# Attention scores made transposed in column halves on TensorE, turned by VectorE in 32x32 blocks, with the row statistics exchanged between partition quarters

## The reference, cut to what matters

```python
q = (query @ wq).reshape(bs, sq, 32, 128)     # query: x, normalised
k = (key @ wk) ...; v = (value @ wv) ...      # key, value: ctx; each kv head serves 4 query heads
q, k = rope(q), rope(k)
raw = einsum('bhqd,bhkd->bhqk', q, k) / sqrt(128) + mask
attn = softmax(raw, axis=-1)                  # over the 64 keys of the same sequence
x = x + tanh(g) * (attn @ v) @ wo
```

## Time and profile before

| | us |
|---|---|
| median of three runs | 782.57 |
| profiled execution, its own time | 782.34 |
| its span (first to last instruction) | 780.5 |
| PE busy | 770.2 |
| DVE busy | 561.7 |
| POOL busy | 498.7 |
| ACT busy | 421.6 |

### The profile page before, as it was taken

The page is one execution under the profiler, slowest core; times in us unless marked ns, Lnnn a source line. Parts: engine busy times, 40 slices in busy tenths (PEclk is TensorE's granted clock), DMA queues, the critical chain, the costliest instruction groups (busy, mean ns, idle before and its releaser), DMA issues.

```text
span 780.5 us, 13547 instructions
## 1 busy us (share of the span) xinstructions
PE 770.2 (99%) x4845; PEld 628.6 (81%) x4845; DVE 561.7 (72%) x1072; ACT 421.6 (54%) x796; POOL 498.7 (64%) x431
## 2 busy tenths in 40 slices
PE   8999999999999999999999999999999999999998
PEld 7888888888888888888888888888656777777776
DVE  6868876677777556677655656656999987998874
ACT  5754454433444433343444324332779898888773
POOL 2798477655567764556776545655377876887752
PEclk9999999999999999999999999999999999999999
DMA  9315645554633343352244311357163323113101
GB/s 338 111 41 136 182 109 133 159 119 120 171 105 105 107 129 103 92 162 86 88 105 133 105 38 55 67 164 280 44 173 96 96 61 93 53 49 82 47 16 41
DMA packets 94798, 85.70 MB, mean 110 GB/s; under 512 B 50652, under 2 KB 66236, under 8 KB 94348
## 3 DMA queue, kind: packets, MB, share of 16 engines
q1 hardware_dynamic: 94444, 84.51, 38.0%
q10 hardware_dynamic: 288, 0.33, 0.1%
HBM read 56.38 MB, written 13.68 MB: 90 GB/s over the span
## 4 chain that ended last, share of the span: by engine, by line
PE 91%; DVE 4%; ACT 1%; POOL 1%; SPq 1%; issue 1%; DMA 0%; DVEq 0%; POOLq 0%
PE bank L81 12%; PE bank L83 11%; PE bank L82 11%; PE bank L583 7%; PE bank L606 7%; PE bank L601 7%; PE bank L602 7%; PE bank L697 4%; PE bank L1699 4%; PE bank L1685 3%; PE bank L1651 2%; PE bank L1630 2%; PE bank L1622 2%; PE bank L1675 2%; PE bank L1676 2%; PE bank L1662 1%
## 5 line engine op out<-in xcount | busy, mean ns | idle before, releaser
L1007 DVE SCALAR_TENSOR_TENSOR x_res<-bank,gate,x_res 128x512 f32<-128x512 f32 x128 | 95.5, 747 | 71.4 <-PE bank L606 70.8
L1278 POOL TENSOR_TENSOR prob<-prob,row_inv 128x512 f32<-128x512 f32 x32 | 33.5, 1046 | 154.6 <-DVE row_inv L996 154.6
L1264 POOL TENSOR_TENSOR rope_swap<-rope_swap,trig 128x512 f32<-128x512 f32 x80 | 104.2, 1302 | 29.2 <-ACT rope_swap L767 28.8
L893 ACT CAST oT_hi<-bank 128x512 fp32r<-128x512 f32 x64 | 34.4, 590 | 162.4 <-PE bank L697 162.4
L766 ACT COPY rope_swap<-bank 64x512 f32<-64x512 f32 x80 | 46.8, 585 | 111.3 <-DVE rope_cos L971 111.3
L601 PE MATMUL bank<-wo_hi,oT_hi 128*128 128x512 f32 x256 | 101.5, 397 | 0.6 <-issue 0.5
L81 PE MATMUL bank<-xnT_hi,wq_hi 128*128 128x512 f32 x252 | 101.7, 404 | 0.0
L602 PE MATMUL bank<-wo_lo,oT_hi 128*128 128x512 f32 x256 | 100.9, 394 | 0.0
L83 PE MATMUL bank<-xnT_hi,wq_lo 128*128 128x512 f32 x252 | 99.7, 395 | 0.0
L82 PE MATMUL bank<-xnT_lo,wq_hi 128*128 128x512 f32 x252 | 99.5, 395 | 0.0
L971 DVE TENSOR_TENSOR rope_cos<-bank,trig 128x512 f32<-128x512 f32 x80 | 54.1, 677 | 56.3 <-PE bank L83 54.1
(11 more groups left out here) (276 smaller groups left out, 1887.7 us busy)
## 6 DMA issues: line engine op xcount, KB each, us to landing
wq_raw<-in_wq_tiles SPq DMA_DIRECT2D x16, 512.0 KB, 3.8
wo_raw<-in_L_xattn_wo SPq DMA_DIRECT2D x16, 512.0 KB, 3.9
blocks_dram<-blocks SPq DMA_DIRECT2D x28, 256.0 KB, 2.0
probT<-blocks_dram SPq DMA_DIRECT2D x112, 64.0 KB, 2.0
xn<-in_L_ffn_Wd SPq DMA_DIRECT2D x16, 256.0 KB, 2.9
b_ctx<-in_ctx SPq DMA_DIRECT2D x32, 128.0 KB, 2.7
b_k_twice<-b_qk_hi SPq DMA_DIRECT2D x32, 128.0 KB, 2.4
w_T_dram<-w_out SPq DMA_DIRECT2D x28, 128.0 KB, 3.1
```

Of the source, the lines that this page charges most:

```text
L1007: dve.scalar_tensor_tensor(out=K.x[:, t, :], in0=wo_ps[t % 2][:, :], scalar=K.gate[:, 0:1], in1=K.x[:, t, :], op0=ALU.mult, op1=ALU.add).t ...
L1264: pool.tensor_tensor(out=sw, in0=sw, in1=sin_b, op=ALU.mult).then_inc(s_rope, 1)
```

## The change

Scores are made the other way round: the keys are stationary (64 columns) and (head, query) moves (128 columns), and the two sequences of a tile go to the two halves of the output partitions. DVE turns the 32x32 blocks of the scores, so that queries (32 of them) lie on partitions and keys along the row, but a query's 64 keys are in two neighbouring partition quarters. Maximum and sum are therefore taken over 32 keys each, and exchanged between neighbouring quarters by four copies of 32 rows x 16 columns, each time followed by a joint maximum or sum. A second turn of the blocks gives the transposed weights directly in `probT`; the transposes on PE and the way through DRAM go. The conversion of weight pieces moves from DVE to ACT, and the order of DVE's and POOL's programs changes: `normalise` stands behind the first rotation, the turn back behind the first accumulation, the low parts of the heads are apart. In slots 0 and 1 PE does items earlier.

```diff
+NROW = HALF // QB
...
-        mask = sb("mask", [P, B, S])
+        mask = sb("mask", [P, UNITS, HALF])
...
-            def blocks_out(U):
...
-            def blocks_in(U):
...
@@ score_unit (PE) @@
-                    pe.wait_ge(s_soft, 5 * (U - 1) + 1)
-                for n in range(2 * UT):
-                    b = 2 * UT * u + n
-                    mm = pe.matmul(score[:, n * S:(n + 1) * S], q_rope[jp][:, b], k_rope[:, b * S:(b + 1) * S],
-                                   start=True, stop=True)
+                    pe.wait_ge(s_soft, soft(U - 1, TURNED))
+                for tl in range(UT):
+                    for par in range(2):
+                        b = 2 * (UT * u + tl) + par
+                        mm = pe.matmul(score[par * S:(par + 1) * S, tl * P:(tl + 1) * P], k_rope[:, b * S:(b + 1) * S],
+                                       q_rope[jp][:, b], start=True, stop=True)
@@ slot (PE) @@
+            def slot(g, last, jp, u, U, items):
+                lead = {0: len(items), 1: 1}.get(U, 0)
+                if U == 1:
+                    item(*items[0])
+                if U > 0:
+                    output(U - 1)
...
+                    score_unit(g if (jp, u) != (1, UNITS - 1) else g + 1, *next_unit(jp, u))
+                if U == 0:
+                    for G, pos in items:
+                        item(G, pos)
+                values(g, jp, u, U)
+                for G, pos in items[lead:]:
                     item(G, pos)
@@ body (ACT) @@
                     if (p := piece_at(2 * U - 1)) is not None:
                         shift(p)
+                        to_int(p)
...
+                    if U > 0:
+                        attended(U)
                     if U < 2 * NPAIR - 1:
                         exp_unit(U + 1)
+                    for G, pos in items[0:1]:
+                        evacuate(G, pos)
...
+                    if (p := piece_at(2 * U)) is not None:
+                        to_int(p)
@@ DVE @@
+            def swap_halves(U, step):
+                dve.wait_ge(s_soft, soft(U, step))
+                for q in range(NQ):
+                    mine, other = slice(q * QB, (q + 1) * QB), slice((q ^ 1) * QB, ((q ^ 1) + 1) * QB)
+                    dve.tensor_copy(row_other[other, U % 2, :], row_max[mine, U % 2, :]).then_inc(s_swap, 1)
             def soft_first(U):
...
+                dve.transpose(pr, score[:, :]).then_inc(s_soft, 1)
+                dve.wait_ge(s_soft, soft(U, TURNED))
+                dve.scalar_tensor_tensor(out=pr, in0=pr, scalar=float(1.0 / np.sqrt(np.float32(DH))), in1=mask[:, u, :],
+                                         op0=ALU.mult, op1=ALU.add).then_inc(s_soft, 1)
+                dve.wait_ge(s_soft, soft(U, MASKED))
+                dve.tensor_reduce(out=row_max[:, u, :], in_=prob[u][:, :, :], op=ALU.max, axis=AX_X).then_inc(s_soft, 1)
+            def soft_shift(U):
+                u = U % 2
+                swap_halves(U, MAX_OWN)
+                dve.wait_ge(s_swap, swapped(U, 1))
+                dve.tensor_tensor(out=row_max[:, u, :], in0=row_max[:, u, :], in1=row_other[:, u, :], op=ALU.max).then_inc(s_soft, 1)
+                dve.wait_ge(s_soft, soft(U, MAX_BOTH))
+                dve.tensor_tensor(out=prob[u][:, :, :], in0=prob[u][:, :, :],
+                                  in1=row_max[:, u, :].unsqueeze(2).to_broadcast([P, NROW, QB]), op=ALU.subtract).then_inc(s_soft, 1)
             def soft_sum(U):
...
+            def soft_inverse(U):
...
+                swap_halves(U, SUM_OWN)
...
+            def turn_back(U):
                 dve.wait_ge(s_prob, U + 1)
+                dve.transpose(probT[:, :, :].rearrange("p t n -> p (t n)"), prob[U % 2][:, :, :].rearrange("p r c -> p (r c)")
+                              ).then_inc(s_probT, 1)
@@ slot (DVE) @@
                 for k in range(UT):
+                    T = UT * (U - 1) + k
+                    accumulate(T, T % NT)
...
+                    if k == 0:
+                        turn_back(U)
+                    if k == 1 and (p := piece_at(2 * U)) is not None:
                         find_scale(p)
...
+                low_heads(U, 0)
+                if U < 2 * NPAIR - 1:
+                    soft_shift(U + 1)
+                for G, pos in items[0:1]:
+                    cosine(G, pos)
+                low_heads(U, 1)
                 if U < 2 * NPAIR - 1:
                     soft_sum(U + 1)
+                if (p := piece_at(2 * U + 1)) is not None:
+                    find_scale(p)
+                if U < 2 * NPAIR - 1:
+                    soft_inverse(U + 1)
...
+                for G, pos in items[1:]:
+                    cosine(G, pos)
@@ body (POOL) @@
-                    if U < 2 * NPAIR - 1:
-                        normalise(U + 1)
                     for k, (G, pos) in enumerate(items):
                         if ITEMS[G][pos][0] != "v":
                             rotate(G, pos)
+                        if k == 0:
+                            normalise(U + 1)
```

More of the change, by code:

```diff
@@ L148, in attention_block @@
         w_scaleT = sb("w_scaleT", [P, QB])
[L149 to L150 removed]
+        row_other = sb("row_other", [P, 2, NROW])
         bank = [cx.ps(f"bank{i}", [P, HALF], F32, st) for i in range(8)]
@@ L291, in attention_block, with soft, swapped @@
         NQP = 2
-        ON_PE = (0, 2 * NPAIR - 3, 2 * NPAIR - 2, 2 * NPAIR - 1)
-        def n_turned(n):
-            return sum(1 if U in ON_PE else NQ * 16 for U in range(n))
+        TURNED, MASKED, MAX_OWN, MAX_BOTH, SHIFTED, SUM_OWN, SUM_BOTH, INVERSE = range(1, 9)
+        def soft(U, step):
+            return INVERSE * U + step
+        def swapped(U, n):
+            return 2 * NQ * U + NQ * n
         block = st.enter_context(nc.Block())
@@ L419, in _ @@
             for V in range(4 * NPAIR):
-                U = V // 2
-                turned = V % 2 == 0 and U not in ON_PE
-                if turned:
-                    blocks_out(U)
                 if (p := piece_at(V + 1)) is not None and p > 0:
@@ L676, in _, with values @@
             item(0, 11)
-            def slot(g, last, jp, u, U, items):
-                if U > 0:
-                    output(U - 1)
-                if U in ON_PE:
-                    pe.wait_ge(s_prob, U + 1)
-                    for tl in range(UT):
-                        mm = pe.transpose(trans[:, tl * P:(tl + 1) * P], prob[u][:, tl], K.ident[:, :])
-                    mm.then_inc(s_probT, 1)
-                if U == 2 * NPAIR - 1:
-                    base_T(1)
-                    base_T(2)
-                if U < 2 * NPAIR - 1:
-                    score_unit(g if (jp, u) != (1, UNITS - 1) else g + 1, *next_unit(jp, u))
-                pe.wait_ge(s_probT_sb, n_turned(U + 1))
+            def values(g, jp, u, U):
+                pe.wait_ge(s_probT, U + 1)
                 if jp == 0 and g % 2 == 0:
@@ L697, in slot @@
                         mm = pe.matmul(av[par][:, tl * P:(tl + 1) * P], v_nat[rows, UT * u + tl, g % 2 * DH:(g % 2 + 1) * DH],
-                                       probT[rows, :, tl, :], start=True, stop=True)
+                                       probT[rows, tl, :], start=True, stop=True)
                 mm.then_inc(s_av, 1)
-                for G, pos in items:
+            def slot(g, last, jp, u, U, items):
[4 more added lines that the diff above has]
+                    output(U - 1)
+                if U == 2 * NPAIR - 1:
+                    base_T(1)
+                    base_T(2)
+                if U < 2 * NPAIR - 1:
[5 more added lines that the diff above has]
+                for G, pos in items[lead:]:
                     item(G, pos)
@@ L832, in shift, with to_int @@
                                ).then_inc(s_p_shift, 1)
+            def to_int(p):
+                kind, w, r, lo, n, rows = PIECES[p]
+                if kind == "max":
+                    return
+                q = n_quant(p)
+                act.wait_ge(s_p_shift, q + 1)
+                if q >= 2:
+                    act.wait_ge(s_p_T[q % 2], 16 * (q // 2))
+                act.activation(w_quant[q % 2][0:rows, 0:n], w_raw[p % 3][0:rows, 0:n], ACT.Copy, bias=-MAGIC
+                               ).then_inc(s_p_quant, 1)
             def qkv_weights():
@@ L875, in prior_logarithm, with attended @@
                 act.activation(M.lsum[0:E_ALL, :], K.log_eps[0:E_ALL, :], ACT.Tanh)
+            def attended(U):
+                act.wait_ge(s_av, U + 1)
+                for par in range(2):
+                    act.copy(oT_hi[:, :, :, par, :], av[par][:, :].rearrange("p (t h q) -> p t h q", t=UT, h=2)
+                             ).then_inc(s_oT_hi, 1)
             def body(g, last):
@@ L1330, in body @@
                             rotate(G, pos)
+                        if k == 0:
+                            normalise(U + 1)
                         if k == (1 if last and len(items) == 2 else 0) and not (last and jp == 1):
```

(4 more changed lines are left out.)

152 lines of the change are left out of this document (54 added, 98 removed).

## The result

The changed kernel takes 795.26 us, the median of 4 runs (794.81 to 796.02); the kernel before, run beside it, 782.48 (781.98 to 782.71). The ratio is 1.0165, with a 95% interval of 1.0148 to 1.0183: slower by 1.65%, where 777 us, slightly faster, was forecast, and outside the range of 764 to 790. The profiled execution took 795.70 us with a span of 793.9, against 782.34 and 780.5 before: 13.4 us of span to explain.

The account below looks back on a forecast made before the run. PE, busy 99% of the span, was taken to bound the kernel. The terms -31 + 14.4 + 6 + 4 + 1 = -5.6 us took 782.34 us to 776.7, say 777; range 764 to 790.

Parts of the forecast that it names:

- Scores on PE: Score matmuls in attention: run side by side, they save 0.91 us a unit, 29.1 us; with PE transposes gone, 31 us.
- The mask addition and the third item: Three-item slots: mask addition waits for POOL's port, 0.9 us late; third item stalls 0.6 in 24 slots, 14.4 us.
- The copies: DVE's exchange copies of 32 rows x 16: 0.17 us each, 0.68 for four (0.5 to 1.2).
- rival B: Exchange copies queue behind POOL's instructions and delay the cosine: 1.0 us stall in 24 slots, 789 us; chance 0.29.
- Its sign, an average over 0.5 us: What would show rival B in the trace: copies of 32 rows averaging over 0.5 us.
- not the bound as a whole: DVE's total work after the change: some 615 us, 79% of the time, though its queue is in order.
- The lead-in … 1 us: Start of attention: unit 0's longer chain with POOL busy, covered by two items, costs 1 us.
- Short slots and the end: Five two-item slots lose some 1.2 us each, 6 us; unit 31's longer chain and later low part cost 4 us.

Follow-up runs that it names:

- experiment 4: The changed kernel with scale and mask applied while the scores are read from PSUM, the turn behind it in SBUF; 788.93 us.
- experiment 3: The changed kernel without the 8 copies per unit and the waits for them, so without the exchange; 768.06 us.
- experiment 2: The changed kernel with each of the 8 copies per unit made by a one-input reduction over an axis of length 1; 782.90 us.
- experiment 6: The changed kernel with the probabilities' turn back behind DVE's third accumulation of a slot instead of its first; 794.74 us.
- experiment 12: The changed kernel with reductions in place of the copies and the mask applied while PSUM is read, all on DVE; 777.36 us.
- experiment 8: The changed kernel with copies on ACT, scale and mask applied while reading PSUM, and the turn back behind the third accumulation; 770.22 us.
- 11: The kernel of experiment 8 with, in unit 30's slot alone, both low parts in front of the exchange and the experts' selection behind it; 770.03 us.

## Why the prediction was wrong

**Scores on PE: right in kind, too large.** The step took 0.91 us per unit, 29 us, and 31 with the PE transposes. Alone, the scores' edit gave 20.7; per slot it is 0.70 (16.99 to 16.29), since the 16 matmuls take 1.02 and about 0.1 is lost in front of them. In the changed kernel the floor of 23 slots is 391.4 - 372.8 = 18.6 lower, 0.81 a slot. This step accounts for 3 to 7 us of the miss.

**The mask addition and the third item: right in kind, too large, and right in the sum by luck.** The instruction and its cause held: 945 ns against 690, and PE waits for ACT's copies out of the bank. The size did not. The step had the mask addition 0.9 late and a stall of 0.6 in each of 24 slots, 14.4 us; it is 0.25 late in the mean (0.54 at most in the middle slots), and taking its wait away gives 6.3 us, 5.3 of them in the 23 middle slots, 0.23 a slot (experiment 4). The stall of those slots is (383.3 - 372.8)/23 = 0.46 in the mean because the copies, which the forecast had at nothing, make about as much again: the reductions take off the same 5.3 us, and both together 9.8. Nor is it in every slot: 7.4 of the 10.5 us are in slots 4, 5, 12, 13, 20 and 21, where a late mask addition and a waiting exchange of maxima (1.68 us) come together. And the middle's -8.1 against -7.1 compares a saving of 18.6 less a stall of 10.5 with 20.9 less 13.8: two terms too large by about the same.

**The copies: failed.** "I take 0.17, so 0.68 for four" is what a free copy costs; the bounds of 0.13 to 0.29 left out a wait for the port, and rival B alone had it. B's mechanism acts as well: 36 of the 64 exchanges meet POOL's instructions and last 1.7 to 3.9 us. Its sign, an average over 0.5 us, was set too high, since 0.386 was enough; and the first exchange, on which B put its stall in all 24 slots, waited in only six of them. What B said against itself, "the second low part is over before the copies come", fails in a middle slot. POOL's timeline of the changed kernel there, and DVE's:

```profile
123.81 1.75 POOL L1268 TENSOR_TENSOR wq_lo<-wq_raw,wq_hi 128x512 fp32r<-128x512 f32 x1
125.52 1.29 POOL L1268 TENSOR_TENSOR wk_lo<-wk_raw,wk_hi 128x512 fp32r<-128x512 f32 x1
```

```profile
123.36 1.04 DVE L993 SCALAR_TENSOR_TENSOR prob<-prob,mask 128x512 f32<-128x512 f32 x1
...
125.75 1.68 DVE L984 COPY row_other<-row_max 32x16 f32<-32x16 f32 x4
```

The slot begins at 115.89, so the second low part ends at slot time 10.9 where 9.5 was forecast (the first one took 1.75 beside the mask addition), and the copies, at 9.9, have 1.06 us of it to wait for. The 256 copies wait 57.6 us in sum, and 12.4 of time come back when they don't. The other 14.8 us that the exchange costs (experiment 3) have no term in the sum either: the forecast counted the copies' 1.36 us a unit as DVE's work and took DVE for "not the bound as a whole". B's 789 was short as well, for the reason below.

**"The lead-in … 1 us": failed, and this is the largest part.** Up to unit 3 the forecast had -0.7, with 1 for unit 0 and 1.2 for each of two short slots; the trace has +13.3. Unit 0's chain was costed as free time under two items. There POOL rotates without a pause, so both its exchanges wait (2.00 and 3.88 us instead of 0.76), unit 0's normalisation stands behind two more rotations, unit 1's exchange (2.82) stands ahead of unit 0's turn back, PE stands for 5.81 and then works at half the clock for 4.1. The clock had no term at all. Slots 0 and 1 take 12.50 and 16.72; the work of slot 0 takes 10.61 at a granted clock of 1.00 (experiment 2), and slot 1 with the same stands 15.15 (experiment 6), so some 3.5 us of the 13.3 are the clock's. Without the exchange unit 3's values still start 3.0 later than before (96.06), with everything moved or reordered 1.7 later (94.74). That the reductions get back little there in some executions is the clock too, in good part: in experiment 12 slot 1 takes 17.48 against 12.90 in experiment 8. 1.8 us of this are longer stands (3.5 against 1.7), and 2.8 are the same work at a granted clock of 0.80 instead of 1.00 (PE busy for 13.97 against 11.17). Why the clock falls behind a stand in some executions and not behind the same stand in others, no run here shows.

**Short slots and the end: right in kind, too small.** The step had 1.2 for each short slot and 4 at the end, and +2.1 for the stretch of units 26 to 31, which came out at +6.8. Against experiment 8, slots 27 to 29 lose (46.77 - 41.89)/3 = 1.6 each, and slot 30 is 4.9 longer than before although it should have been shorter. That chain remains too long without port waits (experiments 8 and 11), and in the changed kernel itself both its exchanges were free. So the term in slot 30 is made of the chain's length, and of the clock that fell with the stand (some 1.6 of the 4.9), and not of the port.

The rest, 1.4 us behind unit 31, was not followed: between the kernels of these experiments that stretch varies from 224.7 to 226.5 without an edit aimed at it.

In short: the mechanism named as the main one was there, at under half of its size (14.4 forecast, 6.3 measured). The sum failed because the same wait, and the exchange's own length, were not charged to the copies (27.2 us in all), because the places with the least cover, the first units and the last, were priced with round numbers instead of a timeline of their own (-0.7 and +2.1 us of change, where the trace has +13.3 and +6.8), and because PE's lower clock after a long stand had no term (some 5 us at the two ends).

## What to carry to other kernels

Where DVE copies tiny tiles in SBUF beside a busy POOL, charge each group of copies with the POOL instructions that run at that time, not with its own length alone; the same exchange as one-input reductions was free of it here, and on ACT it was faster still; an instruction that must have two inputs should take one from PSUM where it can. Write out the timeline of a pipeline's first and last slots as carefully as that of its middle: the chain there has no cover, and here 8 of 32 units decided the sign. Price a long stand of PE with more than its length, since in three places here the matmuls behind it ran at 1.2 GHz for 3 to 5 us. A microsecond saved on the engine that bounds the kernel counts only while the other engines' chains still fit into what is left of the slot: of 20.7 us the changed kernel kept none, and the version with the mask applied first and the copies on ACT kept 11.

## What the runs showed of the hardware

- A copy of 32 rows x 16 in SBUF on DVE takes 161 to 168 ns when free and up to 1245 beside POOL; a reduction of the same shape takes 156 to 167 in all 256 cases.
- Between two copies in a row POOL's next instruction can take the port, as it seems: four copies spanned three POOL instructions (3.88 us), where they take 0.76 when free.
- When the copies stop waiting, the next instruction with two SBUF inputs does: 680 ns instead of 175.
- The same small copy on ACT takes 202 ns in the mean.
- The form that puts two 64-column products side by side ran 16 in 1.02 us, and cost about 0.1 us where it followed full-size matmuls.
- After a stand of 5.81 us PE's granted clock was 0.50 for 4.1 us of work. Behind a stand of 3.20 it fell to 0.50 for some 3.4 us in one execution (the slot took 16.72) and stayed at 1.00 in two others (15.15 and 15.17).
